# Attention scores of two heads by one product over 96 stacked rows, stacked through a scratch in memory, in a gated block with experts

## What is computed

```python
x = x + tanh(g_xattn) * attention(layernorm(x), ctx, ctx)      # 16 heads of 16, causal within 128 tokens
x = x + tanh(g_ffn) * moe(layernorm(x))                         # 8 experts, the best 2 per token, capacity 640
# attention, per head:  scores = (q * 16 ** -0.5) @ k.T, masked;  p = softmax(scores);  o = p @ v;  then @ wo + bo
# moe: layernorm * gamma + beta, logits, softmax, top 2, rank within the expert, silu(g) * u, W3, weighted sum
```

## Time and profile before

| | us |
|---|---|
| three runs | 542.34, 542.40, 545.05 |
| median | 542.4 |
| the profiled execution's own time | 546.42 |
| its span, first to last instruction | 544.5 |
| TensorE busy | 488.8 |
| VectorE busy | 364.9 |
| ScalarE busy | 299.0 |
| GpSimd busy | 208.6 |

### The profile page before, as it was taken

The page is one execution under the profiler, slowest core; times in us unless marked ns, Lnnn a source line. Parts: engine busy times, 40 slices in busy tenths (PEclk is TensorE's granted clock), DMA queues, the critical chain, the costliest instruction groups (busy, mean ns, idle before and its releaser), DMA issues.

```text
span 544.5 us, 10727 instructions
## 1 busy us (share of the span) xinstructions
PE 488.8 (90%) x3529; PEld 452.5 (83%) x3551; DVE 364.9 (67%) x854; ACT 299.0 (55%) x757; POOL 208.6 (38%) x272
## 2 busy tenths in 40 slices
PE   5799999999999887289699899999999999999991
PEld 4588887777777766289599799999999999999991
DVE  6757878889998997547658285376753767644340
ACT  3679878687777753417546273274732646433140
POOL 8535776777878556500020303203031030301212
PEclk9899999899999987779799899999999999999996
DMA  8858422314142611162456536146460555101011
GB/s 265 223 98 261 78 40 71 68 60 79 41 78 58 206 48 51 49 225 108 164 138 205 129 88 175 16 132 186 127 183 10 136 174 138 21 11 19 11 20 19
DMA packets 41649, 57.33 MB, mean 105 GB/s; under 512 B 3721, under 2 KB 38576, under 8 KB 39552
## 3 DMA queue, kind: packets, MB, share of 16 engines
q1 hardware_dynamic: 35168, 48.62, 30.8%
q0 software_dynamic: 6144, 8.07, 8.9%
q10 hardware_dynamic: 288, 0.00, 0.0%
HBM read 36.24 MB, written 16.72 MB: 97 GB/s over the span
## 4 chain that ended last, share of the span: by engine, by line
PE 54%; DVE 1%; DMA 1%; issue 1%; ACT 1%; POOL 1%; POOLq 0%; DVEq 0%
PE bank L1438 17%; PE bank L1439 16%; PE bank L1440 16%; PE bank L1361 2%; PE bank L1432 2%; DMA stage<-in_w3T 1%; ACT wh L714 0%; POOL expert_rows L484 0%; DMA expert_rows<-xr,slotu 0%; PE bank L1304 0%; DVE bXl L1099 0%; POOL out_tokens L546 0%; DVE wl L1092 0%; PE bank L1238 0%; DVE ysc L1142 0%
## 5 line engine op out<-in xcount | busy, mean ns | idle before, releaser
L546 POOL DMA_INDIRECT out_tokens<-ysc,rows x32 | 49.4, 1542 | 254.8 <-DVE ysc L1142 248.3
L1438 PE MATMUL bank<-bXh,wh 128*128 128x384 f32 (+1 forms) x384 | 122.7, 320 | 2.7 <-issue 2.5
L1439 PE MATMUL bank<-bXl,wh 128*128 128x384 f32 (+1 forms) x384 | 122.5, 319 | 0.0
L1440 PE MATMUL bank<-bXh,wl 128*128 128x384 f32 (+1 forms) x384 | 122.4, 319 | 0.0
L749 ACT ACTIVATE sil<-bank 128x384 f32<-128x384 f32 (+1 forms) x96 | 43.7, 456 | 133.1 <-PE bank L1440 133.0
L1121 DVE TENSOR_TENSOR hF<-sil,bank 128x384 f32<-128x384 f32 (+1 forms) x96 | 48.9, 510 | 81.0 <-ACT sil L749 81.0
L633 ACT ACTIVATE p<-bank,nm 128x128 f32<-128x128 f32 x256 | 73.6, 386 | 16.7 <-DVE nm L924 16.7
L1438 PEld LDWEIGHTS bank<-bXh,wh 128*128 128x128 f32 x384 | 73.1, 190 | 3.1 <-issue 3.1
L1438 PE MATMUL bank<-wh,hH 128*128 128x256 f32 x256 | 74.4, 291 | 0.3 <-DVE ysc L1142 0.3
L1440 PEld LDWEIGHTS bank<-bXh,wl 128*128 128x128 f32 x384 | 73.2, 191 | 0.0
L1439 PEld LDWEIGHTS bank<-bXl,wh 128*128 128x128 f32 x384 | 73.1, 190 | 0.0
(11 more groups left out here) (146 smaller groups left out, 884.0 us busy)
## 6 DMA issues: line engine op xcount, KB each, us to landing
stage<-in_w12T SPq DMA_DIRECT2D x16, 1024.0 KB, 4.9
stage<-in_w3T SPq DMA_DIRECT2D x8, 1024.0 KB, 5.6
expert_rows<-padrow SPq DMA_DIRECT2D x8, 662.5 KB, 7.6
rows<-expert_rows SPq DMA_DIRECT2D x7, 662.5 KB, 4.2
kM<-k SPq DMA_DIRECT2D x64, 64.0 KB, 2.4
cT<-in_ctxT SPq DMA_DIRECT2D x8, 256.0 KB, 3.2
out_tokens<-x_all SPq DMA_DIRECT2D x8, 256.0 KB, 2.3
x_all<-in_x SPq DMA_DIRECT2D x2, 640.0 KB, 8.5
```

The source lines that it names most:

```text
L546: pool.indirect_dma_start(out=out, out_offset=bass.IndirectOffsetOnAxis(rows[par][:, c, D + E:ROW].bitcast(U32), 0), in_=ysc[par][:, c, :] ...
L1438: nc.tensor.matmul(out_ap, ah, bh, start=start, stop=False)
L1439: nc.tensor.matmul(out_ap, ah, bl, start=False, stop=False)
L1440: return nc.tensor.matmul(out_ap, al, bh, start=False, stop=stop)
```

## The change

Queries and keys of body 1 and later are put into another form. `qS` has, for each pair of heads, 96 rows: 32 rows of high halves of the query (two heads of 16), the same 32 again, and 32 rows of low halves. `kS` has 32 rows of high halves of the key, 32 of low halves and 32 of high halves, for each of the two heads in its own columns, with zeros in the rows of the other head. One product over the 96 rows gives all three terms for two heads, 256 columns; a group takes two of them. Body 0 keeps the old form (`first_scores`), with `kM` single and the queries in the first part of `qS[0]`.

The stacks are made by DMA through two scratch tensors in memory: `k2` and `q2`, high and low, are sent to `kD` and `qD`, and read back into `kS` and `qS`. For each of the bodies 1 to 7 SP issues four sends of 256 KB, six reads of 128 KB and three reads of 256 KB in place of eight DMAs of 64 KB.

The projections change places: keys go to group 0, input columns to group 1, queries to group 2, on TensorE and ScalarE; on ScalarE the keys stand behind the exponentials of group 0. On GpSimd `normalize_inputs` and `queries_low` move in front of the first norm. What is zeroed is the same in size. The diff, cut to its core:

```diff
+HP = H // 2
+SR = 2 * HD
@@ gated_block
+        qD = nc.dram_tensor("query_halves", (2, P, DC, SB * T), F32).ap()
+        kD = nc.dram_tensor("key_halves", (2, P, DC, SB * T), F32).ap()
-        kM = [sb(pa, f"kM{i}", [P, 2, H, SB * T], F32R) for i in range(2)]
+        kM = sb(pa, "kM", [P, 2, H, SB * T], F32R)
+        kS = [sb(pa, f"kS{i}", [P, HP, 2, SB * T], F32R) for i in range(2)]
-        q2 = [sb(pa, f"q2_{i}", [P, 2, DC, SB * T], F32R) for i in range(2)]
+        qS = [sb(pa, f"qS{i}", [P, HP, SB * T], F32R) for i in range(2)]
+        q0 = qS[0][:, 0:2 * DC, :].rearrange("p (s c) t -> p s c t", s=2)
+        q2 = sb(pa, "q2", [P, 2, DC, SB * T], F32R)
@@ sync
+            def stack_keys(par, part, half):
+                for h in range(2):
+                    r = part * SR + h * HD
+                    sp.dma_start(kS[par][r:r + HD, :, h, :].bitcast(F32).rearrange("d (c a) t -> d c a t", c=DC),
+                                 kD[half].rearrange("(a h d) c t -> h d c a t", h=2, d=HD)[h]).then_inc(ld_k, 16)
+            def stack_queries(par, part, half):
+                sp.dma_start(qS[par][part * SR:(part + 1) * SR, :, :].bitcast(F32).rearrange("r (c a) t -> r c a t", c=DC),
+                             qD[half].rearrange("(a r) c t -> r c a t", r=SR)).then_inc(ld_q, 16)
+            def stack(n, par):
+                sp.wait_ge(act_kT, n + 1)
+                sp.dma_start(kD[0], k2[:, 0, :, :].bitcast(F32)).then_inc(sent_kh, 16)
+                sp.wait_ge(pool_kl, n + 1)
+                sp.dma_start(kD[1], k2[:, 1, :, :].bitcast(F32)).then_inc(sent_kl, 16)
+                sp.wait_ge(sent_kh, 16 * n)
+                stack_keys(par, 0, 0)
+                stack_keys(par, 2, 0)
+                sp.wait_ge(sent_kl, 16 * n)
+                stack_keys(par, 1, 1)
+                sp.wait_ge(act_q, n + 1)
+                sp.dma_start(qD[0], q2[:, 0, :, :].bitcast(F32)).then_inc(sent_qh, 16)
+                sp.wait_ge(pool_ql, n + 1)
+                sp.dma_start(qD[1], q2[:, 1, :, :].bitcast(F32)).then_inc(sent_ql, 16)
+                sp.wait_ge(sent_qh, 16 * n)
+                stack_queries(par, 0, 0)
+                stack_queries(par, 1, 0)
+                sp.wait_ge(sent_ql, 16 * n)
+                stack_queries(par, 2, 1)
@@ turn
-                spread_keys(n, par)
+                    sp.wait_ge(ks_zero[0], 2)
+                stack(n, par)
                 store_x2(n - 2)
@@ gpsimd
             def keys_low(n):
                 pool.wait_ge(act_kT, n + 1)
+                if not (isinstance(n, int) and n < 2):
+                    pool.wait_ge(sent_kl, 16 * (n - 1))
...
@@ gpsimd body
                 if nxt:
                     keys_low(n + 1)
+                if nxt2:
+                    normalize_inputs(n + 2)
+                if nxt:
+                    queries_low(n + 1, q2)
                 if prev1:
                     norm2(n - 1, 0)
                     if cur:
                         normalize2(n - 1, 1 - par, 0, reuse)
-                if nxt2:
-                    normalize_inputs(n + 2)
-                if nxt:
-                    queries_low(n + 1, 1 - par)
@@ scalar body
+                    if g == 7 and nxt:
+                        values(n + 1, Xp)
+                    if cur:
+                        exps(G, g, not prev1 and g < 2)
+                    if g == 0 and nxt:
+                        keys(n + 1, Xp, True)
                     if g == 0 and prev1:
                         output_columns(SB * (n - 1), Xo)
-                    if g == 7 and nxt:
-                        values(n + 1, Xp)
                     if g == 2 and prev2:
                         x2_columns(n - 2, Xo)
-                    if g == 3 and nxt:
-                        keys(n + 1, Xp, True)
-                    if cur:
-                        exps(G, g, not prev1 and g < 2)
...
-                    if g == 4 and nxt:
-                        queries(n + 1, 1 - par, Xp, True)
-                    if g == 0 and nxt:
+                    if g == 2 and nxt:
+                        queries(n + 1, q2, Xp, True)
+                    if g == 1 and nxt:
                         input_columns(n + 1)
@@ tensor
+            def scores(G, g, n, par):
+                b, hq = g // GPS, g % GPS
+                mask(G, g, False)
+                if g == 0:
+                    pe.wait_ge(ld_k, 6 * 16 * n)
+                    pe.wait_ge(ld_q, 3 * 16 * n)
+                for a in range(2):
+                    ins = nc.tensor.matmul(S[g % 2][:, a * 2 * T:(a + 1) * 2 * T].rearrange("p (h t) -> p h t", h=2),
+                                           qS[par][0:3 * SR, 2 * hq + a, b * T:(b + 1) * T],
+                                           kS[par][0:3 * SR, 2 * hq + a, :, b * T:(b + 1) * T],
+                                           start=False, stop=(a == 1))
+                ins.then_inc(pe_s, 1)
@@ tensor body
+                    if g == 2 and prev2:
+                        pe.wait_ge(dve_x2, SB * (n - 1) + 1)
+                        x2_columns(n - 2, par, Xo)
                     if nxt:
-                        if g == 2:
+                        if g == 0:
                             keys(n + 1, 1 - par, Xp, use)
-                        elif g == 4:
+                        elif g == 1:
+                            input_columns(n + 1, False, not prev1)
+                        elif g == 2:
                             queries(n + 1, Xp)
...
-                    if g == 0 and nxt:
-                        input_columns(n + 1, False, not prev1)
```

More of the change, by code:

```diff
@@ L186, in gated_block @@
         act_q32, act_k32, pool_kl, pool_ql = (sem(n) for n in ("act_q32", "act_k32", "pool_kl", "pool_ql"))
[L187 removed]
+        km_zero, ks_zero, ld_km = sem("km_zero"), [sem("ks_zero0"), sem("ks_zero1")], [sem("ld_km0"), sem("ld_km1")]
+        sent_qh, sent_ql, sent_kh, sent_kl, ld_q, ld_k = (sem(n) for n in ("sent_qh", "sent_ql", "sent_kh", "sent_kl", "ld_q", "ld_k"))
         pe_v, pe_bo, dve_bo, act_vf, act_v1, pool_vr, act_v2, pool_v3 = (sem(n) for n in ("pe_v", "pe_bo", "dve_bo", "act_vf", "act_v1", "pool_vr", "act_v2", "pool_v3"))
@@ L271, in _ @@
             pad(range(E // 2))
-            sp.wait_ge(km_zero[1], 3)
-            spread_keys(1, 1)
+            sp.wait_ge(ks_zero[1], 1)
+            stack(1, 1)
             def store_x2(n):
@@ L377, in keys_low, with queries_low @@
                 pool.wait_ge(act_kT, n + 1)
+                if not (isinstance(n, int) and n < 2):
+                    pool.wait_ge(sent_kl, 16 * (n - 1))
                 pool.tensor_tensor(k2[:, 1, :, :], kT[:, :, :], k2[:, 0, :, :].bitcast(F32), ALU.subtract).then_inc(pool_kl, 1)
-            def queries_low(n, par):
+            def queries_low(n, halves):
                 pool.wait_ge(act_q, n + 1)
-                pool.tensor_tensor(q2[par][:, 1, :, :], qT[:, :, :], q2[par][:, 0, :, :].bitcast(F32), ALU.subtract).then_inc(pool_ql, 1)
+                if not (isinstance(n, int) and n < 2):
+                    pool.wait_ge(sent_ql, 16 * (n - 1))
+                pool.tensor_tensor(halves[:, 1, :, :], qT[:, :, :], halves[:, 0, :, :].bitcast(F32), ALU.subtract).then_inc(pool_ql, 1)
             def rstd1(a, b):
@@ L510, in body @@
                     dispatch(n - 2, par)
-            queries_low(0, 0)
+            queries_low(0, q0)
             pool.wait_ge(dve_bo, 1)
@@ L604, in keys @@
                        .then_inc(act_k32, 1)
-                if prev1:
+                if isinstance(n, int) and n == 1:
                     for half in ld_km:
-                        act.wait_ge(half, KM * n)
+                        act.wait_ge(half, KM)
+                elif prev1:
+                    act.wait_ge(sent_kh, 16 * (n - 1))
                 act.wait_ge(act_k32, DC * (n + 1))
@@ L1251, in ranks, with mask @@
                     .then_inc(pe_rk, 1)
-            def scores(G, g, n, par, early):
-                b, hq = g // GPS, g % GPS
-                if g == 0:
-                    pe.wait_ge(pool_ql, n + 1)
-                if g < 2:
-                    pe.wait_ge(ld_km[g], KM * (n + 1))
+            def mask(G, g, early):
                 if not early:
@@ L1310, in body @@
                     G = NG * n + g
-                    if cur:
-                        scores(G, g, n, par, not prev1 and g < 2)
+                    if cur and prev1:
+                        scores(G, g, n, par)
+                    elif cur:
+                        first_scores(g)
                     if g == 7 and prev2:
```

63 lines of the change are left out of this document (35 added, 28 removed).

## The result

Before 543.15 us (median of 4 runs beside it), after 581.08 us (579.45 to 582.5, 4 runs): ratio 1.0697, 95% interval 1.0666 to 1.0728. I had forecast 546.0 with a range of 536 to 554. The profiled execution of after took 579.45 us, its span is 577.8, 33.3 more than before's. Between the medians it is 37.9: before's profiled execution was itself 3.3 over its median, so the traces account for less than the medians.

The account below looks back on a forecast made before the run. A GpSimd and VectorE loop bounds bodies 3 to 6, TensorE bodies 1 and 2. Body 6's second norm shifts +4.6 us, less four times 0.3 returned, +3.4: median 542.4 becomes 545.8, rounded to 546, range 536 to 554.

Parts of the forecast that it names:

- What bounds the kernel before: Bodies 3 to 6 are bound by a loop of GpSimd and VectorE, period 24.37 us; bodies 1 and 2 by TensorE.
- Scores: Score products save TensorE 0.25 us a group, 14 us over bodies 1 to 7; worth nothing in 3 to 7.
- GpSimd's order: Operations moved ahead of the first norm release L948 1.04 us later (bodies 3-5), 1.26 (body 6); 0.3 returned each.
- L948 "held" inside a scatter: In body 7 VectorE's head-output scaling, begun inside GpSimd's last scatter, was still held 3.18 us, contradicting the skill on descriptor generation.
- ScalarE's order: Keys moved to group 0: third value part 8.5 us after group 0 for 7.1 (body 2); covered in bodies 3-6.
- Memory path: Stack reads land 15.2 us after GpSimd's third value part (V); TensorE stands 1.9 us in bodies 3 to 6, costless.
- Body 0 at nothing: Keys ahead of body 0's exponentials cost ScalarE 1.4 us, but these waited anyway: 0, bounds -1 and +1.5.
- the padding rows are through by then: Body 1's stack sends stand behind the padding rows (DMA share 0.81), which were taken to be finished by then.
- Bodies 1 and 2 at 23.7: With no cover there, 8.5 + 15.2 gives 23.7 us a body, for 20.6 and 22.4 before.
- Rival 3: Late stack reads (V+18): TensorE stands 5 us at group 0, 2-3 us a body in six: 557 us; chance 0.10.

Follow-up runs that it names:

- high_only: The kernel before with only the high by high score product, the two products with low halves left out; 540.06 us, ratio 0.9939.
- order_only: The kernel before with the new projection order on TensorE, ScalarE and GpSimd, keeping old scores and spread keys; 547.89 us, ratio 1.0077.
- v_early: The changed kernel with ScalarE's second value part moved to the head of the body, ahead of group 0's exponentials; 578.83 us, ratio 1.0638.
- sp_order: The changed kernel with SP's stack sends and reads issued in the order their halves become ready; 571.37 us, ratio 1.0505.

## Why the prediction was wrong, point by point

- **What bounds the kernel before: right.** high_only moves V4 to V7 by nothing.
- **Scores: right that the relief doesn't reach the time, its price was off.** A group saves 0.45 us at full clock, not 0.25: with 0.22 for the mask, two products of 256 columns take some 0.23 together, the 0.11 each that I had as the lower bound, and I took 0.20. TensorE's busy time fell by 10.2 us in all (488.8 to 478.6), for the 14 forecast, part of it at the lower clock; body 6's is 21.0 us for 22.6. In high_only the relief shows in V0 to V4 and not behind it. In after none of it reaches the time. The weight loads of 96 rows took 190 ns in the median, those of 128 rows 188 before. That agrees with the page of the Trainium skill that I had cited ("TensorE: Matmul & The Clock Gate", LDWEIGHTS): fewer rows load no faster. I had assumed that the loads set the distance of these products, and they didn't.
- **GpSimd's order: right in size, not in condition.** order_only gave L948 let go behind L442, a period of 25.0 for my 25.1 (25.4 less the 0.3 returned), and +3.9 for +3.4. That the totals meet is in part luck: the intervals between V add up to 1.8 only. I missed that GpSimd's order alone opens a gap.
- **L948 "held" inside a scatter: misread.** The row of body 7 (begun at 192.85 inside the scatter of 192.50, held until 196.03) doesn't show a scatter holding it. L948 begun inside a scatter took 0.29 us at 212.04 in before and at 115.42, 140.42 and 165.46 in order_only, each time with another scatter next. What was held at 192.85 had GpSimd's run of tensor operations right behind that scatter. Why it was held ahead of that run's recorded start (193.48) is open. So these traces don't contradict the second half of what the prediction cites there.
- **ScalarE's order, "covered in 3 to 6": wrong in after**, where V waits for ScalarE in six bodies (25.3 us). v_early shows that this was not the cause by itself.
- **Memory path: the step that failed**, in two places. Its terms: query sends through at V+12.7 for my V+10.7, as they were priced at a store's 2.3 us alone but queue behind six key reads (the page of after has 4.7 in the median); the reads issued at V+14.6 for V+12.6; group 0 at V+18.7 for V+15.2, as the reads took 4.1 us behind the last issue and not 2.6. In the other place I let VectorE's stall at L948 absorb the wait, "so it costs nothing". That stall is ended by GpSimd's run, and the operation (L998 in after) took only 0.85 us in this turn, begun at 116.25 with the low keys already done: the wait comes at group 0, ahead of the statistics, the projections and V, and all of them move with it. Thus the period became stack plus group 0 to V, 18.7 + 9.0, a loop that I had written down for bodies 1 and 2 and not tried on 3 to 6. There my own 15.2 + 8.5 = 23.7 lies under 24.4, so both errors were needed. sp_order shows that the stack's timing costs in these bodies, and order_only that without the stack they stand at 25.0. That the way back runs through V is a sum along after's trace only: v_early cut that link, and groups 0 of bodies 2 and 6 came only 1.2 us closer.
- **Body 0 at nothing, "the padding rows are through by then": wrong**, 9.9 us in V0-V1. The high key send was issued at 25.7 behind four padding stores and its reads followed 7 us later; I had not counted what a send meets in engines that are full.
- **Bodies 1 and 2 at 23.7: wrong**, 27.9 us each between the first products of their groups 0 and the next, by the same terms.
- **Rival 3** named the mechanism (late reads, TensorE 5 us at group 0, the lower clock) with the read at V+18, and gave 557: it let GpSimd's cover take 3.3 us of it and charged 2 to 3 us a body. Chance 0.10 was too low for a path with five waits in a row, none of which had a row in the trace.

What stays open: how the 17.0 us lost from V0 to V2, more than half of the traces' difference, split between the stack's depth, the padding stores and the engines' rate; by which branch group 0 leads back to the stack; and the 3.4 us behind V7. The stack was not tried with the padding spread over more bodies, nor by fewer, larger direct transfers.

## What to carry to other kernels

Price a chain of dependent transfers by what stands ahead of each in its queue and engines at that moment, not by what it takes alone, and count its issues. When such a chain ends in what all engines start from, close the loop through every branch before calling a wait covered. Relief of an engine that is not in the loop was worth nothing there (0.45 us of TensorE in each group), while the new dependence was paid in every body.

## What the runs showed of the hardware that I had not expected

- The same 256 KB send took 2.1 us in the median as key halves and 4.7 as query halves, behind six 128 KB reads.
- While those reads and the query sends were under way (119 to 123 us) the engines moved 134 to 143 GB/s at shares of 1.09 and 1.17; with the query reads and the next context load (129 to 131) it was 268 GB/s at 1.11. Nearly the same share went with twice the bytes.
- Eight padding stores took ScalarE's queue 11.8 us to issue and GpSimd's 7.3, while SP's took 3.9 for four.
